# Vision tower in three stages: the order of the routing work in stage one and of the row statistics in stage three is changed

## The reference

```
h = tok(x)                                   # patch embedding, class token, position
h = h + mixer(layernorm(h))                  # inner layernorm, 8 projections of 128, tanh and
                                             # sigmoid gates, 4-tap causal convolution, scan
h = h + ffn(layernorm(h))                    # pooled sums over 1, 2, 4 tokens; layernorm; 3 views with
                                             # gelu; layernorm; 2 of 8 experts per token (128-512-128);
                                             # layernorm
h = h + attn(layernorm(h))                   # 8 heads, keys within 32 tokens
h = h + last(layernorm(h))                   # mean over tokens -> 1 of 16 experts per image (128 x 128)
```

## Time and profile before

| | us |
|---|---|
| median of 3 runs | 2887.75 (2885.34 to 2888.98) |
| profiled execution, its own time | 2891.1 |
| its span | 2888.0 |
| stage one, about | 0 to 1190 |
| stage two, about | 1190 to 1800 |
| stage three, about | 1800 to 2888 |

### The profile page before, as it was taken

The page is one execution under the profiler, slowest core; times in us unless marked ns, Lnnn a source line. Parts: engine busy times, 40 slices in busy tenths (PEclk is TensorE's granted clock), DMA queues, the critical chain, the costliest instruction groups (busy, mean ns, idle before and its releaser), DMA issues.

```text
span 2888.0 us, 71290 instructions
## 1 busy us (share of the span) xinstructions
PE 2576.3 (89%) x25177; PEld 2032.2 (70%) x25177; DVE 2083.3 (72%) x6017; ACT 1803.9 (62%) x3853; POOL 1033.2 (36%) x916
## 2 busy tenths in 40 slices
PE   6998999999898988499999997899999999999996
PEld 4666666666666665399999996676677776667765
DVE  3788888888888888455555554577777777777775
ACT  3777767767777776344444443566766676666674
POOL 1355555555555555455555554101110111000100
PEclk9999999999999999699999998999999999999998
DMA  3222222222222211377777775121112211122110
GB/s 136 70 83 84 85 83 82 83 83 89 87 98 84 87 60 35 107 233 229 228 235 228 228 233 171 39 67 51 51 51 61 65 51 51 51 62 62 51 34 29
DMA packets 135788, 288.40 MB, mean 100 GB/s; under 512 B 22752, under 2 KB 79072, under 8 KB 131424
## 3 DMA queue, kind: packets, MB, share of 16 engines
q1 hardware_dynamic: 113504, 245.36, 27.9%
q0 software_dynamic: 22016, 39.43, 4.2%
HBM read 215.79 MB, written 68.92 MB: 99 GB/s over the span
## 4 chain that ended last, share of the span: by engine, by line
PE 62%; DVE 20%; ACT 12%; issue 4%; DMA 1%; POOL 1%; SPq 0%; DVEq 0%; ACTq 0%; POOLq 0%
PE psum L513 15%; PE psum L1190 9%; PE psum L1181 9%; PE psum L519 4%; PE psum L1592 3%; PE psum L1535 3%; PE psum L1552 3%; ACT nrows L1752 3%; PE psum L1540 2%; ACT ex L1788 2%; DVE acc L816 2%; PE psum L1605 2%; PE psum L1575 2%; ACT r L1758 2%; ACT r L1760 2%
## 5 line engine op out<-in xcount | busy, mean ns | idle before, releaser
L1225 ACT ACTIVATE hid<-psum,w_blk 128x256 f32<-128x256 f32 x608 | 268.9, 473 | 325.0 <-PE psum L1181 325.0
L1047 POOL DMA_INDIRECT expert_in<-rows,slot_i x384 | 376.7, 981 | 157.0 <-issue 140.6
L1788 ACT ACTIVATE ex<-psum,smin 128x80 f32<-128x80 f32 x1152 | 281.1, 331 | 206.9 <-DVE smin L1874 206.8
L1153 POOL DMA_INDIRECT expert_out<-rows_out,dest x304 | 291.0, 957 | 290.5 <-DVE rows_out L1320 242.3
L513 PE MATMUL psum<-xn,w_in 128*128 128x288 f32 x1024 | 313.5, 432 | 31.6 <-ACT rf L726 27.6
L1190 PE MATMUL psum<-w_blk,hid 128*128 128x128 f32 x2432 | 297.2, 276 | 0.0
L1181 PE MATMUL psum<-x_t,w_blk 128*128 128x256 f32 x1216 | 289.6, 382 | 2.2 <-DMA w_blk<-w_exp_in 2.2
L1190 PEld LDWEIGHTS psum<-w_blk,hid 128*128 128x128 f32 x2432 | 284.4, 193 | 0.1
L1514 POOL TENSOR_TENSOR x2c<-x2c,ycho 96x768 f32<-96x768 f32 x32 | 57.7, 1802 | 611.4 <-DMA ycho<-expert_out 611.4
L513 PEld LDWEIGHTS psum<-xn,w_in 128*128 128x128 f32 x1024 | 192.0, 200 | 99.3 <-DVE xn L874 40.4
L1017 POOL TENSOR_TENSOR unit<-unit 128x576 f32<-128x576 f32 x64 | 120.0, 1875 | 354.9 <-ACT unit L680 272.7
(11 more groups left out here) (259 smaller groups left out, 5789.8 us busy)
## 6 DMA issues: line engine op xcount, KB each, us to landing
w_blk<-w_exp_in SPq DMA_DIRECT2D x152, 578.5 KB
xin<-x_in SPq DMA_DIRECT2D x32, 1716.0 KB, 7.1
rows_in<-expert_in SPq DMA_DIRECT2D x152, 132.0 KB
ycho<-expert_out SPq DMA_DIRECT2D x64, 288.0 KB, 5.3
h_dram<-h SPq DMA_DIRECT2D x32, 288.0 KB, 2.1
x_dram<-rows SPq DMA_DIRECT2D x32, 288.0 KB, 3.2
h1c<-h_dram SPq DMA_DIRECT2D x32, 288.0 KB, 4.4
x2c<-x_dram SPq DMA_DIRECT2D x32, 288.0 KB, 5.2
```

What stands on the lines that cost most here:

```text
L1047: pool.indirect_dma_start(out=expert_in[:, :], out_offset=bass.IndirectOffsetOnAxis(ap=slot_i[z.s][:, n:n + 1], axis=0), in_=rows[z.s][:, ...
L1153: pool.indirect_dma_start(out=expert_out[:, :], out_offset=bass.IndirectOffsetOnAxis(ap=dest[b.s][:, c:c + 1], axis=0), in_=rows_out[b.s][ ...
L1225: nc.scalar.activation(hid[b.s][:, c, :], HB[b.s][c % HK], ACT.Gelu_apprx_tanh, bias=w_blk[b.q][:, FF + FC * D + c:FF + FC * D + c + 1]).t ...
L1788: done = nc.scalar.activation(ex[u][:, b, in_window(qb)], score_bank(u)[:, b * QK:(b + 1) * QK], ACT.Exp, bias=smin[u % RING][:, b:b + 1], ...
```

## The change

Stage one. variance3 goes to bank A0 in place of B0, so that unit 0 need not wait for its evacuation, and instead waits for both multiplies of norm 0. The Squares of norms 3 and 1 stand behind the Exps of norm 0 and ahead of the Ln of norm 3, and norm 1 gets buffers of its own (`sq`, `ra`). The rank products move behind variance2, and on VectorE `route_ranks` and `route_slots` move to the end of the step.

Stage three. `ysum` and `halves3` get a second buffer; `row_halves` moves from the step of item w to the end of the step before and is split in two, `normed_rows` is split in two as well and stands behind norm 5. `moe` uses A0 and stands behind turn 3 and values 2, `router` uses A1, `centre` of h2 stands right behind `router` and waits for the first step of `pick_expert`, and values 4 follows the averaging product of norm 4.

```diff
@@ -613,17 +613,19 @@
     pe.wait_ge(squared3, z.upto(1, 1))
-    project(B0, C("mean"), sqf[:]).then_inc(variance3, 1)
+    if x:
+        pe.wait_ge(normed, x.upto(2, 2))
+    project(A0, C("mean"), sqf[:]).then_inc(variance3, 1)
 if x:
     pe.wait_ge(normed, x.upto(2, 1))
-    if z:
-        pe.wait_ge(logvar3, z.upto(1, 1))
     unit_in(x, 0, B0)
...
         pe.wait_ge(normed, x.upto(2, 2))
-    project(A0, C("mean"), sqf[:]).then_inc(variance1, 1)
+    if z:
+        pe.wait_ge(logvar3, z.upto(1, 1))
+    project(A0, C("mean"), sq[:]).then_inc(variance1, 1)
 if x:
@@ -651,10 +653,6 @@
     unit_in(x, 4, B0)
-if z:
-    if x:
-        pe.wait_ge(unit_act, x.upto(8, 4))
-    ranks(z, A1)
 if x:
@@ -666,6 +664,10 @@
     project(B0, C("mean"), sqf[:]).then_inc(variance2, 1)
+if z:
+    if x:
+        pe.wait_ge(unit_act, x.upto(8, 4))
+    ranks(z, A1)
@@ -713,20 +715,20 @@
     nc.scalar.activation(two(ra[:]), both(B1), ACT.Ln, bias=eps_col[:, 0:1]).then_inc(logvar0, 1)
-if z:
-    act.wait_ge(centered3, z.upto(1, 1))
-    nc.scalar.activation(two(sqf[:]), both(A1), ACT.Square, bias=shift1[:, 0:1]).then_inc(squared3, 1)
 if x:
...
 if z:
+    act.wait_ge(centered3, z.upto(1, 1))
+    nc.scalar.activation(two(sqf[:]), both(A1), ACT.Square, bias=shift1[:, 0:1]).then_inc(squared3, 1)
+if y:
+    act.wait_ge(centered1, y.upto(1, 1))
+    nc.scalar.activation(two(sq[:]), both(B1), ACT.Square).then_inc(squared1, 1)
+if z:
     act.wait_ge(variance3, z.upto(1, 1))
-    nc.scalar.activation(two(rf[:]), both(B0), ACT.Ln, bias=eps_col[:, 0:1]).then_inc(logvar3, 1)
-if y:
-    act.wait_ge(centered1, y.upto(1, 1))
-    nc.scalar.activation(two(sqf[:]), both(B1), ACT.Square).then_inc(squared1, 1)
+    nc.scalar.activation(two(rf[:]), both(A0), ACT.Ln, bias=eps_col[:, 0:1]).then_inc(logvar3, 1)
 if z:
@@ -734,11 +736,9 @@
     act.wait_ge(variance1, y.upto(1, 1))
-    if z:
-        act.wait_ge(x2_step, z.upto(2, 1))
-    nc.scalar.activation(two(rf[:]), both(A0), ACT.Ln, bias=eps_col[:, 0:1]).then_inc(logvar1, 1)
+    nc.scalar.activation(two(ra[:]), both(A0), ACT.Ln, bias=eps_col[:, 0:1]).then_inc(logvar1, 1)
     act.wait_ge(logvar1, y.upto(1, 1))
-    nc.scalar.activation(rf[:], rf[:], ACT.Exp, scale=-0.5).then_inc(rstd1, 1)
+    nc.scalar.activation(ra[:], ra[:], ACT.Exp, scale=-0.5).then_inc(rstd1, 1)
 act.preload_act_table_set("gelu_apprx_tanh_and_others")
@@ -881,7 +881,7 @@
 v.wait_ge(rstd1, y.upto(1, 1))
-v.tensor_tensor(two(x0[:]), both(B1), two(rf[:]), ALU.mult).then_inc(pool_step, 1)
+v.tensor_tensor(two(x0[:]), both(B1), two(ra[:]), ALU.mult).then_inc(pool_step, 1)
 v.wait_ge(pool_step, y.upto(3, 1))
@@ -918,12 +918,8 @@
     delta(x, 1)
-if z:
-    route_ranks(v, z, A1)
 if x:
     tap(x, 1, 2)
-if z:
-    route_slots(v, z)
 if y:
@@ -932,7 +928,9 @@
 if z:
+    route_ranks(v, z, A1)
     route_weights(v, z)
+    route_slots(v, z)
@@ -1349,8 +1347,8 @@
 h1c, x2c = pair_c("h1c", [128, T]), pair_c("x2c", [G, NG, D])
-ycho, ysum = pair_c("ycho", [G, 2, NG, D]), one_c("ysum", [G, NG, D])
-halves3, stats = one_c("halves3", [G, NG, 6]), one_c("stats", [G, NG, 2])
+ycho, ysum = pair_c("ycho", [G, 2, NG, D]), pair_c("ysum", [G, NG, D])
+halves3, stats = pair_c("halves3", [G, NG, 6]), one_c("stats", [G, NG, 2])
 root3, move3, nrows = one_c("root3", [G, NG]), one_c("move3", [G, NG]), one_c("nrows", [G, NG, D])
@@ -1513,9 +1511,9 @@
 pool.wait_ge(ysum_step, x.upto(YSUM, 1))
-if x.old(1):
-    pool.wait_ge(nrows_ready, x.upto(1, 0))
-pool.tensor_tensor(ysum[:], x2c[x.s][:], ycho[x.s][:, 1, :, :], ALU.add).then_inc(ysum_step, 1)
+if x.old(2):
+    pool.wait_ge(nrows_ready, x.upto(2, -2))
+pool.tensor_tensor(ysum[x.s][:], x2c[x.s][:], ycho[x.s][:, 1, :, :], ALU.add).then_inc(ysum_step, 1)
@@ -1541,7 +1539,7 @@
 def moe(x, bank):
-    pe.wait_ge(nrows_ready, x.upto(1, 1))
+    pe.wait_ge(nrows_ready, x.upto(2, 2))
     for g in range(NG):
@@ -1690,41 +1688,38 @@
     scores(x, 4)
+    turn(x, 3)
+    values(x, 2)
 if w:
     if y:
-        pe.wait_ge(xm_ready, y.upto(1, 1))
+        pe.wait_ge(norm5_act, y.upto(3, 2))
     elif x:
-        pe.wait_ge(val_ready, x.upto(NV, 2))
-    moe(w, A1)
-if x:
-    turn(x, 3)
-    values(x, 2)
+        pe.wait_ge(k_ready, x.upto(1, 1))
+    moe(w, A0)
 if x:
...
 if y:
-    router(y, A0)
+    router(y, A1)
+if w:
+    pe.wait_ge(h2_ready, w.upto(1, 1))
+    if y:
+        pe.wait_ge(pick_step, y.upto(PICK, 1))
+    elif x:
+        pe.wait_ge(val_ready, x.upto(NV, 2))
+    centre(A1, w, h2).then_inc(norm4_pe, 1)
 if x:
...
 if w:
-    pe.wait_ge(h2_ready, w.upto(1, 1))
-    centre(A1, w, h2).then_inc(norm4_pe, 1)
+    pe.wait_ge(norm4_act, w.upto(3, 1))
+    project(A0, C("mean"), sq4[:]).then_inc(norm4_pe, 1)
 if x:
...
     turn(x, 5)
-if w:
-    if y:
-        pe.wait_ge(pick_step, y.upto(PICK, 1))
-    elif x:
-        pe.wait_ge(k_ready, x.upto(1, 1))
-    pe.wait_ge(norm4_act, w.upto(3, 1))
-    project(A0, C("mean"), sq4[:]).then_inc(norm4_pe, 1)
-if x:
     scores(x, 8)
     turn(x, 6)
-if x:
     values(x, 5)
@@ -1744,12 +1739,12 @@
-def normed_rows(x):
+def normed_rows(x, k):
     act.wait_ge(moved_ready, x.upto(1, 1))
...
         act.wait_ge(moe_done, x.upto(1, 0))
-    for g in range(NG):
-        last = nc.scalar.activation(nrows[:, g, :], ysum[:, g, :], ACT.Identity, bias=move3[:, g:g + 1],
+    for g in range(k * NG // 2, (k + 1) * NG // 2):
+        last = nc.scalar.activation(nrows[:, g, :], ysum[x.s][:, g, :], ACT.Identity, bias=move3[:, g:g + 1],
                                     scale=root3[:, g:g + 1])
@@ -1818,35 +1813,38 @@
     exps(x, 1)
+if x:
+    turned(x, 0)
 if w:
     row_root(w)
-if x:
-    turned(x, 0)
 if y:
...
     exps(x, 2)
+if y:
+    inverse_root(y, r5, A0, norm5_pe, norm5_act)
+if x:
+    turned(x, 2)
 if w:
-    normed_rows(w)
-if y:
-    inverse_root(y, r5, A0, norm5_pe, norm5_act)
-if x:
-    turned(x, 2)
+    normed_rows(w, 0)
+if x:
     exps(x, 3)
+if w:
+    normed_rows(w, 1)
 if x:
...
     exps(x, 5)
-    turned(x, 4)
 if w:
...
 if x:
+    turned(x, 4)
     exps(x, 6)
-    turned(x, 5)
 if w:
...
 if x:
+    turned(x, 5)
     exps(x, 7)
@@ -1889,25 +1887,26 @@
-            def row_halves(x):
...
-                v.wait_ge(ysum_step, x.upto(YSUM, YSUM))
-                for g in range(NG):
-                    last = v.bn_stats(halves3[:, g, :], ysum[:, g, :])
+            def row_halves(x, k):
...
+                if k == 0:
+                    v.wait_ge(ysum_step, x.upto(YSUM, YSUM))
+                for g in range(k * NG // 2, (k + 1) * NG // 2):
+                    last = v.bn_stats(halves3[x.s][:, g, :], ysum[x.s][:, g, :])
                 last.then_inc(halves3_ready, 1)
...
             def row_stats(x):
-                v.wait_ge(halves3_ready, x.upto(1, 1))
+                v.wait_ge(halves3_ready, x.upto(2, 2))
                 if x.old(1):
...
                 for g in range(NG):
-                    last = v.bn_aggr(stats[:, g, :], halves3[:, g, :])
+                    last = v.bn_aggr(stats[:, g, :], halves3[x.s][:, g, :])
                 last.then_inc(stats_ready, 1)
...
                 if x.old(1):
-                    v.wait_ge(nrows_ready, x.upto(1, 0))
+                    v.wait_ge(nrows_ready, x.upto(2, 0))
                 v.scalar_tensor_tensor(out=move3[:], in0=stats[:, :, 0], scalar=-1.0, in1=root3[:], op0=ALU.mult,
@@ -1943,15 +1942,13 @@
     pick_gate(v, z)
-if w:
-    row_halves(w)
 if y:
...
     heads(y, 8)
+if x:
+    minimum(x, 1)
 if w:
     row_stats(w)
-if x:
-    minimum(x, 1)
 if z:
@@ -1981,26 +1978,28 @@
     v.tensor_reduce(means[:], four(xm[:]), AX_X, ALU.add).then_inc(means_ready, 1)
-if x:
-    minimum(x, 5)
 if w:
...
     v.wait_ge(h_landed[w.s], 16 * w.n + 16)
-    v.scalar_tensor_tensor(out=two(h2[:, w.s * T:(w.s + 1) * T]), in0=both(A1), scalar=V("ln3_g"),
+    v.scalar_tensor_tensor(out=two(h2[:, w.s * T:(w.s + 1) * T]), in0=both(A0), scalar=V("ln3_g"),
                            in1=two(h1c[w.s][:]), op0=ALU.mult, op1=ALU.add).then_inc(h2_ready, 1)
 if x:
+    minimum(x, 5)
     halves(x, 3)
...
     pick_expert(v, y)
+if v_:
+    row_halves(v_, 0)
 if x:
     halves(x, 4)
-if z:
-    residual(z)
-if x:
     heads(x, 4)
     minimum(x, 7)
+if z:
+    residual(z)
+if v_:
+    row_halves(v_, 1)
 if w:
@@ -2015,7 +2014,7 @@
 v.wait_ge(router_done, x.upto(1, 1))
-v.scalar_tensor_tensor(out=l16[:], in0=A0[0:NI, 0, 0:E2], scalar=1.0 / S, in1=RR("bg")[0:NI, :],
+v.scalar_tensor_tensor(out=l16[:], in0=A1[0:NI, 0, 0:E2], scalar=1.0 / S, in1=RR("bg")[0:NI, :],
                        op0=ALU.mult, op1=ALU.add).then_inc(pick_step, 1)
```

More of the change, by code:

```diff
@@ L724, in step @@
                 if z:
-                    act.wait_ge(variance3, z.upto(1, 1))
-                    nc.scalar.activation(two(rf[:]), both(B0), ACT.Ln, bias=eps_col[:, 0:1]).then_inc(logvar3, 1)
+                    act.wait_ge(centered3, z.upto(1, 1))
```

(15 more changed lines are left out.)

## The result

The changed kernel takes 3042.74 us (median of 4, 3036.11 to 3053.32) against 2887.68 (2885.34 to 2888.98): 1.0541 of the kernel before, 95% interval 1.051 to 1.0573, +155 us. The forecast was 2921, its range ended at 2955.

What follows compares the result with a forecast made beforehand. TensorE has work for 904.45 of 1,000 us in stage one, where VectorE's chain sets the step, and 869.34 of 950 in stage three. Stage one -24 and stage three +57 give +33 us: 2921 us, range 2868 to 2955.

Steps and rivals of the forecast that it cites:

- the sum: Stage three: one serial chain through the engines adds up to a step of 35.0 us against 32.48, 2.5 more.
- a discount from 2.5 to 1.9 us: Stage three: not all of the summed 2.5 us a step need come, so 1.9 was taken, +57 us in 30 steps.
- Unit 0 no longer waits: Stage one: the 0.92 us wait for variance3's Ln goes, variance3 waits 0.1 for xn1; 0.8 us a step gained.
- The ranks' wait moves to squared2: Stage one: TensorE waits ahead of variance2 instead of at the ranks; 0, bounds gain 0.25, loss 0.4 us a step.
- Stage three's chain: Stage three: query, turn 2, exps 3, values 2, logits, centre4, values 4 and xq run serially; 2.5 us a step more.
- Rival 1: Stage three: both GpSimd adds hold the att multiply, about 0.7 us a step more, total +54 us, 2942; chance 0.12.
- Rival 3: Stage three: centre4 doesn't wait for the logits, the tail stays hidden, total -39 us, 2849; chance 0.15.
- rival 2: Stage one gives nothing, as ScalarE's five passes just fill their gap; total +57 us, 2945; chance 0.08.
- rival 4: Stage three loses only its lower bound, 0.5 to 1.0 us a step, near cancelling stage one; 2885 us; chance 0.10.

Runs made afterwards that it cites:

- a_bank: Kernel before plus stage one's new bank for variance3, order of Squares and Exps, sq and ra, ranks at their old place: 2870.60 us, 0.9947.
- a_ranks: Kernel before with only ranks, route_ranks and route_slots moved late in stage one: 2904.26 us, 1.0059 of the kernel before.
- a_fill2: Stage-one part alone plus four unread products ahead of variance2's wait for squared2: 2885.26 us, 1.0005 of the kernel before.
- c_lock: Stage-three part alone, but GpSimd starts its two adds only when att of unit 8 is done: 2988.32 us, 1.0354 of the kernel before.
- c_only: Kernel before with the stage-three part of the change alone: 3016.71 us, 1.0445 of the kernel before.
- c_fill: Stage-three part alone plus unread products, four ahead of turn 3's wait and three ahead of centre4's: 2993.35 us, 1.0369 of the kernel before.
- c_turn: Stage-three part alone, but both halves of the normed rows stand behind exps 3 on ScalarE: 2981.89 us, 1.0321 of the kernel before.
- c_centre: Stage-three part alone, but centre4 and mean4 at their old places on TensorE: 2996.80 us, 1.0377 of the kernel before.
- c_tail: c_centre with ScalarE's old order around norm 4 as well: 3039.38 us on a slower chip, 1.0145 of the kernel before there.
- c_three: Stage-three part alone with the edits of c_lock, c_turn and c_centre together: 3063.42 us on a slower chip, 1.0190 of the kernel before there.
- c_four: c_three with ScalarE's old order around norm 4 as well: 3007.25 us on a slower chip, 1.0042 of the kernel before there.
- a_only: Kernel before with the stage-one part of the change alone: 2903.22 us, 1.0062 of the kernel before; repeated, 2908.75 us, 1.0080.
- best_fill2: a_bank with GpSimd's adds held until att of unit 8, and four unread products ahead of the ranks' wait: 2855.66 us, 0.9900.
- a_fill: Same kernel as a_fill2 on a slower chip that waits at the logits: 3038.76 us, 1.0110 of the kernel before there.
- best_fill: Same kernel as best_fill2 on a slower chip that waits at the logits: 2990.48 us, 0.9950 of the kernel before there.

## Why the prediction was wrong

The direction was right, the size was not: +33 us forecast, +155 measured. The step that failed is the pricing of TensorE's waits by their length alone: the sum puts TensorE's work behind them at its old time, and that work took 1.5 us more a step in stage three. In stage one it is the whole loss of 0.8 us a step: the 8 of 27 steps at full clock average 34.86 us, as those of the kernel before do. To this come a discount from 2.5 to 1.9 us, where 2.4 of idle time came, and the wait behind GpSimd's adds, which stood in a rival and not in the sum.

1. *Unit 0 no longer waits: -0.8 us a step.* Right in kind. The wait is gone, and a_bank is faster by 17 us (24 forecast), of which stage one accounts for 10. Its step at full clock averages 34.35 us against 34.86 before, 0.5 in place of 0.8; variance3 waits up to 0.45 us for xn1, where I allowed 0.1.
2. *The ranks' wait moves to squared2: 0, bounds -0.25 and +0.4 a step.* The wait moved as described (1.77 us). This is the step that failed in stage one, because I costed an idle time by its length alone. a_ranks' steps at full clock average 35.29 us, 0.43 more than before: the upper bound. The rest, to 0.68 over all steps, is the clock: its mean falls from 0.972 to 0.962. With both parts together it is 0.953, and a_fill2 got 24 us back by keeping it up. Stage one, forecast at -24 us, came to +26. The earlier trace rows had shown a clock of 0.97 in this stage, and I read it as a given.
3. *Stage three's chain: 2.5 us summed, 1.9 taken.* The chain was right, link by link but for the first: in the step shown (query at 2317.86, the next at 2353.64, all at a clock of 1.00) the way to the end of turn 2 takes 18.86 us (forecast 18.23, without the wait for `gdiag`), values 2 to the logits 4.63 (4.64), the logits to values 4 4.43 with the handover (4.28), and values 4 to the end of xq 3.61 (3.62). The three of 27 steps at full clock average 35.48 us, where the sum gave 35.0. Over all of them TensorE's idle time per step went from 2.80 to 5.18 us, +2.4. The discount to 1.9 rested on no row and was wrong.
4. *What the sum left out:* TensorE's work at a lower clock. Its busy time per step went from 30.04 to 31.54 us, +1.5, with the same instructions. 2.4 + 1.5 = 3.9 us against the 1.9 taken; over 30 steps +117 and not +57.
5. *Rival 1 (the adds hold att): +0.7.* The mechanism came, at another place. In the step shown the adds start 6.1 us after the query product (2323.96 against 2317.86), where they began 8.45 us after it before (2243.34 - 2234.89), and so they hold att 7 and then gdiag, not att 8. Per step TensorE waits 1.04 us for att and gdiag, where it waited 0.48 for att (25.6 and 13.2 us in 900): about 0.6 more, near the rival's price, to which I gave a chance of 0.12. c_lock's 28 us are more than this difference, because they hold what the kernel before paid as well. It is not on top of points 3 and 4 but a part of them. The Trainium skill ("SBUF — State Buffer", section "Who interferes with whom") names both kinds of VectorE instruction: with two SBUF inputs, and `tensor_scalar` in a mode that uses both ports. This trace agrees in that both ended with the add beside them: att took 1.37 us and gdiag 1.31, where each takes 0.22 otherwise. Whether gdiag ran in such a mode no view shows.
6. *Rival 3 (the logits are no wait)* is refuted by the 1.77 us at centre4; *rival 2* by a_bank; *rival 4* by c_only.

The parts of stage three overlap: c_fill, c_lock, c_turn and c_centre gave back 23, 28, 35 and 20 us singly, and c_tail 0.030 of the time. Three of them nearly add up (c_three: 0.0255 of 0.0283), but c_lock, c_turn and c_tail, 0.052 together, gave 0.040 in c_four. They are cuts through one chain, so a sum of single gains isn't safe. Open is what makes the clock fall in one step and not in the next, when both have the same waits, and why unchanged code of stage three takes up to 13 us less behind some versions of stage one.

## What to carry to other kernels

Cost a wait of TensorE twice: by its length, and by what the work behind it takes at half clock; a stretch whose granted clock is already below 1.00 is a warning that more waits will cost more than their length. When an item is moved in one engine's queue, move its partners in the other queues with it, or the old order waits there. When a sum from rows gives 2.5, take 2.5: a discount needs a row too.

## What the runs showed of the hardware

- Idle times of TensorE of 1.8 to 2.3 us are followed in many steps by several us at a granted clock of 0.50, and in c_four waits of 0.8 and 1.1 us in 17 of 27 steps, while in c_three steps with 4.39 us of idle time kept the clock in 25 of 27. Such a fall cost 1.5 us of TensorE's time in c_four (29.68 against 31.16 us for the same 523 instructions), 1.0 in a step of stage one of before (31.09 against 32.08), and 2.8 in a_only, where it lasted twice as long (31.38 against 34.16).
- Products that nobody reads, 1.7 us of them in the wait, kept the clock at 1.00 in 27 of 27 steps in a_fill2 and best_fill2. On the chip with the wait at the logits they did so in 10 (a_fill) and 18 (best_fill) of 27.
- GpSimd's adds also held a `tensor_scalar` of 4x4 elements: 1.316 us at the median in the changed kernel, against 0.220 in c_lock, where the adds start later.
- Two chips ran the kernel before 4% slower; in the six profiles taken there stage one waited for at most 2.5 to 3.6 us at the logits, for which the profile names no cause.
